# Routed second FFN on one Trainium2 core: per-tile gather and scatter-add replaced by rows pushed into a region per expert, 64 fixed units of 192 slots, and a gather per token

## What is computed

```python
def _L1_ffn_ref(hidden_states, gate_w, w_gate, w_up, w_down):
    x = hidden_states.reshape(-1, 256)                 # T = 1024 tokens
    probs = jax.nn.softmax(x @ gate_w, axis=-1)        # 64 experts
    top_vals, top_idx = jax.lax.top_k(probs, 8)
    top_vals = top_vals / jnp.sum(top_vals, axis=-1, keepdims=True)
    rw = jnp.zeros((T, 64)).at[jnp.arange(T)[:, None], top_idx].set(top_vals)
    g = jnp.einsum('th,ehi->tei', x, w_gate)           # w_gate 64 x 256 x 96
    u = jnp.einsum('th,ehi->tei', x, w_up)
    h = jax.nn.silu(g) * u * rw[:, :, None]
    return jnp.einsum('tei,eih->th', h, w_down)        # w_down 64 x 96 x 256
...
x = x + jnp.tanh(g_ffn[1]) * _L1_ffn_ref(_layernorm(x, axis=-1), ...)
```

## Time and profile before

| | before |
|---|---|
| median of three runs | 486.61 us |
| the profiled execution, span from first to last instruction | 484.2 us |
| mean granted TensorE clock | 0.843 |
| PE matmul / weight load busy | 333.1 / 276.9 us |
| DVE / ACT / POOL busy | 241.1 / 206.3 / 292.6 us |
| indirect DMAs on POOL | 96 gathers, 96 scatters |
| HBM read / written | 47.78 / 17.17 MB |

### The profile page before, as it was taken

How to read it: one execution, slowest core, us unless ns; L and a number is a source line. 1 busy time by engine, 2 the same in 40 slices (tenths; PEclk the granted TensorE clock), 3 DMA queues, 4 the chain that set the end, 5 groups by cost and what they waited for, 6 DMA issues and landing times.

```text
span 484.2 us, 10739 instructions
## 1 busy us (share of the span) xinstructions
PE 333.1 (69%) x2285; PEld 276.9 (57%) x2286; DVE 241.1 (50%) x971; ACT 206.3 (43%) x812; POOL 292.6 (60%) x255
## 2 busy tenths in 40 slices
PE   5894481574343977689787988869667888878630
PEld 2432480474232866578676777758656777767520
DVE  0999999866885434433333434344434433433102
ACT  2254433174652544453444445344445444444320
POOL 3820130232124578788787878787887878888760
PEclk9999996688555899987879779797999887879985
DMA  4900000000055588777787888887878877888858
GB/s 119 373 24 0 2 1 0 2 1 0 1 167 143 123 182 174 166 160 157 165 184 172 169 174 176 170 167 180 172 155 158 165 167 173 181 171 168 178 73 271
DMA packets 68771, 65.19 MB, mean 135 GB/s; under 512 B 10640, under 2 KB 64400, under 8 KB 68752
## 3 DMA queue, kind: packets, MB, share of 16 engines
q0 software_dynamic: 18432, 25.18, 32.1%
q1 hardware_dynamic: 50320, 39.80, 27.7%
HBM read 47.78 MB, written 17.17 MB: 134 GB/s over the span
## 4 chain that ended last, share of the span: by engine, by line
DMA 24%; PE 20%; DVE 20%; issue 19%; POOL 7%; ACT 5%; POOLq 1%; DVEq 1%; SPq 1%; another core or an unknown queue 1%; ACTq 0%
DMA expert_sums<-y_slots,scatter_at 17%; PE psum L691 6%; DMA x_slots<-normed_rows,gather_at 5%; POOL expert_sums L481 5%; DVE work L970 4%; DVE top L966 4%; PE psum L681 3%; PE psum L673 2%; PE psum L698 2%; DVE stats L941 2%; POOL x_slots L472 2%; PE psum L517 2%; PE psum L511 2%; PE psum L607 1%; DMA adj<-expert_sums 1%
## 5 line engine op out<-in xcount | busy, mean ns | idle before, releaser
L481 POOL DMA_INDIRECT expert_sums<-y_slots,scatter_at x96 | 159.1, 1657 | 33.5 <-issue 27.9
L1152 DVE TENSOR_TENSOR h_t<-silu,psum 96x128 f32<-96x128 f32 x96 | 27.2, 283 | 193.1 <-ACT silu L888 81.7
L472 POOL DMA_INDIRECT x_slots<-normed_rows,gather_at x96 | 96.5, 1005 | 38.8 <-issue 18.7
L681 PE MATMUL psum<-ident,x_slots 128*128 128x128 f32 x192 | 51.6, 355 | 50.5 <-DMA x_slots<-normed_rows,gather_at 44.5
L673 PEld LDWEIGHTS psum<-cols,one_hot 128*128 128x128 f16 x768 | 61.9, 165 | 27.2 <-issue 18.1
L691 PE MATMUL psum<-x_slots_t,wg 128*96 128x128 f32 x384 | 69.5, 311 | 8.8 <-issue 6.1
L698 PE MATMUL psum<-wd,h_t 96*128 96x256 f32 x192 | 67.1, 435 | 4.2 <-issue 3.4
L691 PE MATMUL psum<-x_slots_t,wu 128*96 128x128 f32 x384 | 66.4, 302 | 0.0
L1146 DVE TENSOR_TENSOR one_hot<-slot_id,local 128x1024 f16<-128x1024 f16 x96 | 65.7, 685 | 0.0
L673 PE MATMUL psum<-cols,one_hot 128*128 128x4 f16 x768 | 59.6, 199 | 6.7 <-DVE one_hot L1146 5.4
L691 PEld LDWEIGHTS psum<-x_slots_t,wg 128*96 128x96 f32 x384 | 55.7, 190 | 14.2 <-issue 10.7
(11 more groups left out here) (146 smaller groups left out, 436.5 us busy)
## 6 DMA issues: line engine op xcount, KB each, us to landing
wg<-in_L_ffn_w_gate SPq DMA_DIRECT2D x96, 96.0 KB
wu<-in_L_ffn_w_up SPq DMA_DIRECT2D x96, 96.0 KB
wd<-in_L_ffn_w_down SPq DMA_DIRECT2D x96, 96.0 KB
gu_w<-in_L_ffn_gate_up_proj SPq DMA_DIRECT2D x4, 512.0 KB, 8.1
x_slots<-normed_rows,gather_at POOLq DMA_INDIRECT x96
expert_sums<-y_slots,scatter_at POOLq DMA_INDIRECT x96
xs<-in_x SPq DMA_DIRECT2D x1, 1024.0 KB, 5.6
down_w<-in_L_ffn_down_proj SPq DMA_DIRECT2D x4, 256.0 KB, 8.1
```

The source lines that it names most:

```text
L472: pool.indirect_dma_start(x_slots[:, tile.lane, :], None, xn_dram, bass.IndirectOffsetOnAxis(ap=gather_at[:, tile.lane:tile.lane + 1], axi ...
L481: pool.indirect_dma_start(sums_dram[n], bass.IndirectOffsetOnAxis(ap=scatter_at[:, tile.lane:tile.lane + 1], axis=0), y_slots[:, tile.lane ...
L681: last = pe.transpose(psum[:, 2 + tile.two, k * P:(k + 1) * P], x_slots[:, tile.lane, :].rearrange("p (n k) -> p k n", k=KC)[:, k, :], ide ...
L1152: dve.tensor_tensor(h1_t[:, tile.two], silu1[:, tile.two], psum[0:I1, 4 + tile.two, P:2 * P], ALU.mult).then_inc(h_ready, 1)
```

## The change

The new kernel turns the last layer from expert tiles with lists into a push, a fixed loop and a pull.

- **Push.** HBM holds `expert_rows` with a region of 1152 rows for each of 64 experts. For each batch, PE ranks the chosen rows (`rank_rows`), and DVE turns expert and rank into eight row numbers for each token (`place_rows`, DVE). POOL then writes each token tile eight times by an indirect DMA, once for each of a token's experts: 8 tiles x 8 = 64 pushes of 128 rows of 1 KB, plain writes. The pushes stand between and behind the last `inverse_deviation` calls.
- **Units.** A unit is 192 slots, as 2 x 96 (`SUBS`, `SLOTS`). Units 0 to 62 are the first 192 rows of experts 1 to 63, in a loop unrolled in Python; SP loads their rows by a plain DMA (`load_rows`), the weights of gate and up by one DMA and of down by another (`load_weights`), and stores the results as a block (`store_rows`). Expert 0 and whatever an expert has above 192 rows are done after it, in a `Fori` loop of at least one pass; with 169 as the largest count it has exactly one pass.
- **Pull.** When all results are stored, POOL gathers for each token tile its eight result rows (64 indirect DMAs of 128 rows), PE sums them with eight diagonal matrices of the routing weights (`diag`), and DVE adds `x3`.
- Slot lists, `one_hot`, list copies, gathers and scatters in the loop, the two HBM sums and the stores of `x3` and `xn` go. The rows of `expert_rows` that a unit reads (64 x 192) and the spare part of `y_rows` (43 x 192) are zeroed early by two DMAs from SP. The concatenation of gate and up weights is made before the launch.

```diff
+SLOTS = 96
+SUBS = 2
+CAP = SLOTS * SUBS
+W_RING = 8
+X_RING = 4
+Y_RING = 4
+K_RING = 4
...
@@ sync
+            def load_weights(e):
+                n = e % W_RING
+                need(sp, y_filled, e - W_RING + 1)
+                sp.dma_start(wgu[:, n].rearrange("p k n -> p (k n)"), w_gate_up[(e + 1) % NE]).then_inc(w_landed[n], 16)
+                sp.dma_start(wd[:, n], w_down[(e + 1) % NE]).then_inc(w_landed[n], 16)
+
+            def load_rows(e):
+                n = e % X_RING
+                need(sp, xt_filled, e - X_RING + 1)
+                sp.dma_start(x_slots[0:SLOTS, n].rearrange("p i d -> p (i d)"),
+                             x_units[e + 1, 0:CAP * D].rearrange("(p n) -> p n", p=SLOTS)).then_inc(x_landed[n], 16)
+
+            def store_rows(e):
+                n = e % Y_RING
+                sp.wait_ge(y_ready, e + 1)
+                sp.dma_start(y_units[e].rearrange("(p n) -> p n", p=SLOTS),
+                             y_slots[0:SLOTS, n].rearrange("p i d -> p (i d)")).then_inc(y_stored[n], 16)
...
+            for b in range(B):
+                sp.wait_ge(placed[b], 16 * HB * TOP_K_EXPERTS)
+            for e in range(X_RING):
+                load_rows(e)
+            for e in range(UNITS):
+                if e + W_RING <= UNITS:
+                    load_weights(e + W_RING)
+                if e + X_RING < UNITS:
+                    load_rows(e + X_RING)
+                store_rows(e)
...
@@ gpsimd
-            def slot(tile, left):
-                if not first(tile):
-                    scatter(tile.before())
-                if follows(left, AHEAD):
-                    gather(tile.later(AHEAD))
+            place_rows(0, 0, 2)
+            inverse_deviation(2, 2)
+            place_rows(0, 2, 4)
+            inverse_deviation(2, 3)
+            place_rows(0, 4, 10)
+            inverse_deviation(3, 2)
+            place_rows(0, 10, 13)
+            inverse_deviation(3, 3)
+            place_rows(0, 13, PICKS)
+            for b in range(1, B):
+                place_rows(b, 0, PICKS)
...
+            pool.wait_ge(y_stored[LAST_X], total_over * 16 + Y_STORED[LAST_X])
+            pool.sem_inc(over_begun, 1)
+            pool.wait_ge(y_at_ready, 1)
+            for t in range(NT):
+                need(pool, picks_summed, t - K_RING + 1)
+                for k in range(TOP_K_EXPERTS):
+                    pool.indirect_dma_start(picks[t % K_RING][:, k * D:(k + 1) * D], None, y_dram,
+                                            bass.IndirectOffsetOnAxis(ap=y_at[:, t, k:k + 1], axis=0)).then_inc(picks_landed[t % K_RING], 16)
...
@@ tensor
+            transpose_slots(0)
+            transpose_slots(1)
+            for e in range(UNITS):
+                gate_up1(e)
+                if e:
+                    down1(e - 1)
+                if e + 2 < UNITS:
+                    transpose_slots(e + 2)
+            down1(UNITS - 1)
...
@@ vector, order of the front part
             choose_experts(0)
             choose_experts(1)
+            place_rows(0)
+            place_rows(1)
             for b in (2, 3):
                 add_layer0(b)
                 statistics(2, b)
...
+            choose_experts(2)
             router_weights(0)
+            place_rows(2)
+            choose_experts(3)
             router_weights(1)
-            for b in (2, 3):
-                choose_experts(b)
-                router_weights(b)
+            place_rows(3)
```

More of the change, by code:

```diff
@@ L653, in _ @@
             last.then_inc(bank_filled, 1)
-            begin(F_RANK)
-            rank_ps = bank(F_RANK).rearrange("p (t e) -> p t e", t=NT)
-            pe.matmul(rank_ps, before[:], chosen[:], start=True, stop=False)
-            for t in range(NT - 1):
-                last = pe.matmul(rank_ps[:, t + 1:NT, :], ones_b[:], chosen[:, t:t + 1, :].to_broadcast([P, NT - 1 - t, NE]),
-                                 start=False, stop=t == NT - 2)
-            last.then_inc(bank_filled, 1)
-            begin(F_TILES)
@@ L677, in transpose_slots @@
[L677 to L689 removed]
+            begin(F_OVER)
@@ L693, in gate_up1 @@
                 last.then_inc(gu_filled, 1)
-            def down1(tile):
-                pe.wait_ge(h_ready, tile.j + 1)
-                need(pe, y_ready, tile.j - 1)
-                pe.matmul(psum[:, 6 + tile.two, 0:D], h1_t[:, tile.two, :], wd[:, tile.lane, :],
-                          start=True, stop=True).then_inc(y_filled, 1)
-            def slot(tile, left):
-                gate_up1(tile)
-                if not first(tile):
-                    down1(tile.before())
-                if follows(left, AHEAD):
-                    slot_lists(tile.later(AHEAD))
-                if follows(left, 2):
-                    transpose_slots(tile.later(2))
@@ new lines, in _ @@
+            pe.wait_ge(y_ready, total_over + UNITS)
+            pe.sem_inc(over_begun, 1)
+            for t in range(NT):
+                pe.wait_ge(diag_ready, t + 1)
+                pe.wait_ge(picks_landed[t % K_RING], 16 * TOP_K_EXPERTS * (t // K_RING + 1))
+                for k in range(TOP_K_EXPERTS):
+                    last = pe.matmul(psum[:, t, 0:D], diag[:, t % 2, k, :], picks[t % K_RING][:, k * D:(k + 1) * D],
+                                     start=k == 0, stop=k == TOP_K_EXPERTS - 1)
+                last.then_inc(picks_summed, 1)
@@ L1161, in _ @@
-            for n in range(AHEAD):
-                prepare(Tile(0, 0).later(n), load_expert(Tile(0, 0).later(n)))
-            up_times_silu1(over_tiles(dve, slot))
-            for c in range(B):
-                tiles = slice(c * HB, (c + 1) * HB)
-                dve.wait_ge(sums_loaded[c], 16 * N_SUMS)
-                dve.tensor_tensor(xs[:, tiles], base[:, tiles], adj[:, tiles], ALU.add).then_inc(out_ready, 1)
+            link(dve.tensor_scalar(n_over_i[:, 0], n_over[:], 683.0, None, ALU.mult))
@@ new lines, in _ @@
+            link(dve.tensor_tensor(rank[:], rank[:], chosen[:], ALU.mult))
+            for b in range(B):
+                for t in tiles_of(b):
+                    for k in range(TOP_K_EXPERTS):
+                        last = dve.scalar_tensor_tensor(out=picked[:, t % 4, k], in0=order[:, t], scalar=float(TOP_K_EXPERTS - k), in1=rank[:, t],
+                                                        op0=ALU.is_equal, op1=ALU.mult, accum_out=y_pick[:, t, k:k + 1])
+                link(last)
+            dve.tensor_copy(y_at[:], y_pick[:]).then_inc(y_at_ready, 1)
```

625 lines of the change are left out of this document (331 added, 294 removed).

## The result

| | before | changed |
|---|---|---|
| median (lowest to highest), six executions each | 486.36 us (484.8 to 488.47) | 577.69 us (569.9 to 584.62) |
| ratio | 1 | 1.183 (1.175 to 1.190) |
| span of the profiled execution | 484.2 us | 582.9 us |
| mean granted TensorE clock | 0.843 | 0.798 |

The forecast was 537 us, with a range to 574. The direction was right, the size not: 91 us slower instead of 51. The profiled execution of the changed kernel, at 584.6 us, is the slowest of its six.

A forecast was written before the change was run, and what follows sets the result against it. GpSimd's indirect DMAs were taken to bound the kernel, at least 3.18 us a tile. Seven stages in series reached 534.8 us against a span of 484.2; with 2.4 us from span to median, 537 us, range 496 to 574.

The forecast's parts named there:

- Step 1: Routing and placing of batch 0 until the first push: at 117.0 us.
- Step 2: The 64 pushes at 1.35 us each, 86.4 us, plus 5.5 us of other work and waiting: over at 208.9 us.
- second rival: GpSimd locked out by VectorE: pushes at 1.78 us, the pull perhaps at 1.45, 574 us in all; 14%.
- step 4: Loop of units, 62 at 3.25 us plus 2 us for the start and 3.8 for the finish: over at 423.2 us.
- Step 3: From last push to first matmul: landing 2.7 us, load of rows 2.8, transposes and copy 1.5: at 215.9 us.
- cover: During the pushes: VectorE's selections and slipped routing stay hidden unless routing slips by over 20 us.
- circle: In the loop, rows wait for an earlier down product: two units take 3.7 + 2.7 us, one 3.2.
- L: In the loop, from down(e) over two weight issues to the landing of unit e + 4's rows: 3.7 us.
- My 2 us for half clock: Added to the loop of units for a start with TensorE at half clock: 2 us.
- Steps 5 to 7: Expert 0 alone 15.3 us, to 439.5; the pull's 64 gathers 82.6, to 522.1; the end 12.7, to 534.8 us.
- first rival: Loads arrive before TensorE wants them in the loop: a unit takes 2.7 us, 34 us less, 503 us; 22%.
- third rival: Cheap indirect DMAs: the 0.30 us fall away in pushes and pull, and units take 2.7 us: 459 us, faster; 9%.

The follow-up runs named there:

- unaltered: The changed kernel run again with nothing edited: 539.35 us, 1.115 of before; in later sets 542.4, 543.3, 541.8 and 536.9 us.
- rows first: Changed kernel with the load of unit e+4's rows issued ahead of unit e+8's weights in SyncE's loop: 490.8 us, 1.013 of before.
- rows one place later: Changed kernel with the load of unit e+4's rows issued behind the store of unit e: 559.0 us, 1.149 of before.
- rows two ahead: Changed kernel with the rows of unit e+5, instead of e+4, loaded ahead of the weights of unit e+8: 476.3 us, 0.982 of before.
- three experiments: Changed kernel with selections moved into the loop (538.4 us), a semaphore increment behind each push and gather (539.9), or at most four pushes on their way (542.9).

## Why the prediction was right or wrong

By its own steps, in the time of a profiled execution:

| step | forecast | first profile | unaltered, later |
|---|---|---|---|
| 1 first push | 117.0 | 115.4 | 115.5 |
| 2 last push over | 208.9 | 201.0 | 201.8 |
| 3 first gate product | 215.9 | 232.8 | 207.4 |
| 4 units over | 423.2 | 467.6 | 426.7 |
| 5 first gather | 439.5 | 484.6 | 443.7 |
| 6 last gather over | 522.1 | 572.1 | 523.8 |
| 7 end | 534.8 | 582.9 | 534.3 |

**Step 1** held. **Step 2** ended 7 us early, 1.5 of them from step 1: a push takes 0.96 us and 0.30, 1.26 in all, not 1.35. VectorE beside it slows it by some 3%: in the unaltered kernel's profile the 40 pushes beside a VectorE that was busy for over half of them took 1.00 us in the mean, the other 24 0.97. The second rival, 1.78, is out. The rule that I had weighed came nearer than I did. The Trainium skill, SBUF — State Buffer, section "Who interferes with whom", says that `tensor_tensor` does not stop descriptors from being written, which gave 1.29; the row gives 1.26. In the pull, where it lets `tensor_scalar` take the shared pair, the 12 gathers of that profile beside `build_diag` took 0.97 us in the mean and 1.06 at most, the other 52 0.95. That is a tenth of a microsecond now and then, not the second rival's 1.45.

**The forecast failed in two steps.** Of the 48.1 us by which the first profile is over the forecast's 534.8, step 4, the units, has 27.5 (234.8 us instead of 207.3), the time up to the first gate product has 16.9, and the rest 3.7. Either of the first two alone would have stayed inside the range.

**Step 3**, the first gate product, was late because a cover was missing that step 2 had counted on. VectorE's new work "ends before that and hides", the cover gone "only if routing slipped by over 20 us". It slipped by more: L687 ran at 186.1 us instead of 150.6, the selections ended at 231 us, and the first gate product came at 232.8 instead of 207.4, 25 us. The prediction had asked which work covers the selections, not what is exposed when VectorE stands still. Why it stood still is open. Later, without gaps, the selections ended at 178 us, ahead of the rows' landing, and step 3 was 8.5 us early: 1.5 from step 1, 5.6 from step 2 and 1.4 of its own.

**Step 4** is the mis-sized term, in every execution. The circle was right, L + TensorE's unit over two, and TensorE's 2.7 us is 2.73. But L is 4.15 us, not 3.7, because rows land 3.2 us after their issue where the sum had left 2.6 (3.7 less 0.1 and two issues). So (4.15 + 2.73) / 2 = 3.44 us instead of 3.2. The unaltered kernel's loop took 214.0 us over 62 units from copy to copy, 3.45; the profiles of the other sets lie between 3.42 and 3.63. Against my 3.25 that is 12 us. The Trainium skill, DMA: Bandwidth & Descriptors, section "Anatomy of one DMA — SWDGE (gpsimd) path", made it 2.45 us for 196 KB and a unit of 3.1, an estimate, by a fit for DMAs that GpSimd issues, while these come from SyncE. The weights of the same size do land in 2.4 us, and so do rows alone (2.51 us for expert 0 in the first profile, after the loop). In the loop the rows do not, and it is the rows that count. Their place in SyncE's queue is not the reason. These are their medians when they are issued first (rows first), third (unaltered) and last (rows one place later):

```profile
gu_w<-expert_rows SPq DMA_DIRECT2D x64, 192.0 KB, 3.7
gu_w<-expert_rows SPq DMA_DIRECT2D x64, 192.0 KB, 3.3
gu_w<-expert_rows SPq DMA_DIRECT2D x64, 192.0 KB, 3.2
```

They go with what the DMA engines moved from 240 to 360 us, 250, 193 and 173 GB/s, and with the rows two ahead it is 4.0 us at 271 GB/s. Some of the late ones have a neighbour in common. In the loop the trace has eight loads of 16 KB of the program's own instructions; in the unaltered kernel's profile the 8 loads of rows that were on their way at one of them, or issued within 0.5 us after its start, took 3.91 us in the mean and 5.33 at most, the other 51 took 3.27. The eleven other later profiles show the same sign. That is a coincidence in time and not a test of the cause.

TensorE's own unit was too long, too. "It cannot be less than 2.7", says the prediction, but the kernel with the rows two ahead does one in 2.48 us. On the unaltered timeline four transposes without a wait take 0.33 us instead of the 0.53 of the sum.

In the first profile a unit took 3.70. The clock explains a part: 0.95 in its loop, 0.99 in the later one. A wait for rows can cost twice, as in the unaltered kernel's timeline:

```profile
246.67 1.03 PE L718 MATMUL psum<-proj_t,gu_w 96*96 96x256 f32 x4
...
250.43 0.90 PE L698 MATMUL psum<-ident,gu_w 96*128 96x96 f32 x4 [2.73 <-DMA gu_w<-expert_rows]
251.12 2.76 PE L709 MATMUL psum<-gu_w,wgu 128*96 128x192 f32 x8
```

TensorE stood idle for 2.73 us, and the next gate and up products took 2.76 us where they take 1.47 on the same timeline at full clock. My 2 us for half clock covered only the start of the loop. Between the first and the 63rd copy TensorE was at half clock for 23 us in the first profile, for 6 us here. The 17 us more would cost 8 us at most, an estimate (at half clock the same work takes twice as long), of the 15.5 that this loop is longer. But the loops of the unaltered kernel's later profiles, without gaps, spread too: 212 us with 7 us at half clock, 219 with 15, and 225 with 18. So most of the first loop's extra time needs no gaps; the rest I did not isolate.

**Steps 5 to 7** held: expert 0 alone took 17.0 us (16.3 forecast), the pull 80.1 (82.6), the end 10.5 (12.7). In the first profile the pull and the end took 7.7 us more, with gaps of the same kind.

So the later executions, 537 to 542 us, agree with 537, but partly by luck: 8.5 us too much in front of the loop and 4 behind it stand against 12 too little in it. The first measurement's 577.7 is 38 us above the unaltered kernel's 539.35. In the profiled executions, 582.9 against 534.3, the 48.6 us are 25.4 before the first gate product, 15.5 in the loop, and 7.7 in the pull and end. The sums of the range are a few us off (a unit of 3.0 to 3.6 us gives 521.5 to 558.7, not 519 to 561), which changes nothing. The first rival (503) named the right lever: with the order of two loads changed, the rows arrive in time, and the kernel takes 491 us and 476. The last beats the kernel before without what the third rival had asked for: the pushes keep their 0.30 us.

## What to carry to other kernels

When a stage is paced by a circle, write the links out from the chain of waits and ask which of them only an order in a queue puts there: here a load stood behind a wait that it did not need, and moving it was worth 63 us, more than the 54 that the change loses without the gaps. A ring of four buffers helps only as far ahead as the issuing queue runs; compare the issue's place with the moment at which the slot comes free. And before one explains the excess over a forecast by the program, the same program should run again: three experiments here were priced against a delay that the same program did not show again. It also pays to ask whether a profile's record is whole where one reads a wait from it; a view of issues without landing times was the sign here.

## What the runs showed of the hardware

In the first profile VectorE went on 6 to 33 us after the work that it waited for was done, between 146 and 205 us, where the pushes ended at 201, and in the pull; in none of the twelve later profiles. The record of semaphores has its holes in these stretches, 284 of some 1070 steps and 341 of 1152. The 0.30 us between two indirect DMAs are there with nothing, with a semaphore increment and with a wait between them, and no longer for it. Half a microsecond in SyncE's order cost 17 us of the whole, and the 271 GB/s of the fastest loop were no limit. A load of 192 KB of rows took 2.5 us alone and 3.2 to 4.0 us in the loops, more as they moved more. After an idle time of 2.73 us TensorE's next gate and up products ran at half clock, 2.76 us instead of 1.47.
